# A fused decoder layer: mask order, small differences and key sums in its first attention

## The reference

```python
def _feature_map(t, K):
    f = jnp.einsum('hdf,bhld->bhlf', K, t)
    feats = jnp.concatenate([jax.nn.softmax(f, axis=-1), jax.nn.softmax(-f, axis=-1)], axis=-1)
    return jnp.maximum(feats, EPS)          # EPS = 1e-12

def _L0_attn_ref(x, Wq, Wk, Wv, Wo, Kq, Kk):   # 16 heads of 64
    q, k, v = _heads(x @ Wq), _heads(x @ Wk), _heads(x @ Wv)
    qf, kf = _feature_map(q, Kq), _feature_map(k, Kk)
    kv = jnp.cumsum(kf[:, :, :, None, :] * v[..., None], axis=2)
    o = jnp.einsum('bhlf,bhldf->bhld', qf, kv)
    z = jnp.einsum('bhlf,bhlf->bhl', qf, jnp.cumsum(kf, axis=2)) + EPS
    return (o / z[..., None]).transpose(0, 2, 1, 3).reshape(B, L, H * HD) @ Wo

x = x + _L0_attn_ref(_layernorm(x), ...)
x = x + _L0_xattn_ref(_layernorm(x), ctx, mask, ...)
x = x + _L0_ffn_ref(_layernorm(x), ...)
```

## Time and profile before

| | us |
|---|---|
| median of 2 runs | 1312.96 (1311.81 and 1314.12) |
| the profiled execution | 1310.69 |
| its span, first to last instruction | 1308.5 |
| the steady loop of the first attention in it | about 86 to 598 |

### The profile page before, as it was taken

The page is one execution under the profiler, slowest core; times in us unless marked ns, Lnnn a source line. Parts: engine busy times, 40 slices in busy tenths (PEclk is TensorE's granted clock), DMA queues, the critical chain, the costliest instruction groups (busy, mean ns, idle before and its releaser), DMA issues. The chain is left out here.

```text
span 1308.5 us, 30248 instructions
## 1 busy us (share of the span) xinstructions
PE 1151.0 (88%) x11860; PEld 755.3 (58%) x11861; DVE 934.6 (71%) x1705; ACT 645.9 (49%) x1230; POOL 528.8 (40%) x477
## 2 busy tenths in 40 slices
PE   6688795888778898888899999999999975999996
PEld 6577675777667786776334434433444332666665
DVE  6867775776646766667877977787788746677766
ACT  3333343333333343333577867776778852444443
POOL 4464477455644455551331032023100134566651
PEclk9888898888988898999999999999999987999998
DMA  6100002000040000022284058017322017121125
GB/s 226 38 7 2 2 2 73 2 1 1 1 75 2 1 2 1 2 35 43 75 142 88 8 91 153 2 29 125 74 85 116 2 51 201 50 64 64 60 61 196
DMA packets 60046, 73.66 MB, mean 56 GB/s; under 512 B 14404, under 2 KB 51140, under 8 KB 59188
## 3 DMA queue, kind: packets, MB, share of 16 engines
q1 hardware_dynamic: 56132, 61.56, 19.7%
q0 software_dynamic: 3792, 10.36, 2.6%
HBM read 52.86 MB, written 18.78 MB: 55 GB/s over the span
## 5 line engine op out<-in xcount | busy, mean ns | idle before, releaser
L1751 ACT ACTIVATE pt<-pR 128x512 f32<-128x512 f32 x512 | 286.2, 600 | 76.2 <-PE pR L1642 71.3
L1836 DVE TENSOR_REDUCE neg_max<-pS 128x1 f32<-128x1024 f32 x238 | 284.8, 1219 | 52.5 <-PE pS L1619 52.4
L1642 PE MATMUL pR<-qs,ks 100*32 100x512 bf16 x2048 | 190.1, 381 | 2.6 <-ACT pt L1751 1.6
L1619 PE MATMUL pS<-ks,qs 100*32 100x512 bf16 x1904 | 144.9, 378 | 4.8 <-DVE neg_max L1836 1.8
L1656 PE MATMUL b_pO<-pt,b_v 128*32 128x512 f32 x1024 | 134.2, 598 | 2.9 <-ACT pt L1751 2.3
L1498 POOL COPY qs<-max_rows 3x512 bf16<-3x512 bf16 x60 | 36.5, 609 | 209.1 <-ACT max_rows L1744 206.0
L352 POOL TENSOR_TENSOR am<-am,a_causal 128x512 f32<-128x512 f32 x64 | 82.6, 1291 | 70.9 <-ACT am L793 70.9
L1642 PEld LDWEIGHTS pR<-qs,ks 100*32 100x32 bf16 x2048 | 55.9, 96 | 94.1 <-issue 23.9
L543 PE MATMUL pO<-v,am 128*64 128x66 f32 x1024 | 64.5, 237 | 34.4 <-POOL am L352 34.4
L1619 PEld LDWEIGHTS pS<-ks,qs 100*32 100x32 bf16 x1904 | 51.2, 96 | 72.9 <-issue 35.4
L540 PE MATMUL pO<-state,qfT 128*64 128x66 f32 x768 | 52.0, 233 | 39.6 <-POOL am L352 39.4
(11 more groups left out here) (380 smaller groups left out, 2530.2 us busy)
## 6 DMA issues: line engine op xcount, KB each, us to landing
qs<-q_scr SPq DMA_DIRECT2D x24, 256.0 KB
ks<-k_scr SPq DMA_DIRECT2D x7, 768.0 KB
k_scr<-f SPq DMA_DIRECT2D x18, 256.0 KB, 3.0
ks<-in_L_ffn_w_dram SPq DMA_DIRECT2D x2, 2048.0 KB, 11.1
ks<-in_L_ffn_w_dram SPq DMA_DIRECT2D x4, 1024.0 KB, 9.1
ks<-y_rows SPq DMA_DIRECT2D x16, 256.0 KB, 5.0
ks<-k_scr SPq DMA_DIRECT2D x6, 512.0 KB
cx<-in_ctx_dram SPq DMA_DIRECT2D x3, 768.0 KB, 13.0
```

Source lines behind the costliest of these rows:

```text
L1619: ins = pe.matmul(pS1[q:q + XV, slot, 512 * half:512 * half + 512], qs[0:KR, bass.ds(par, 1), h, P * t + q:P * t + q + XV].rearrange("r a ...
L1642: ins = pe.matmul(ring[bank][q:q + XV, :], ks[0:KR, bass.ds(par, 1), h, P * j + q:P * j + q + XV].rearrange("r a n -> r (a n)"), qs[0:KR, ...
L1751: nc.scalar.activation(pt[:, j % 2, i, :], ring[bank], ACT.Exp).then_inc(exp_done, 1)
L1836: nc.vector.tensor_reduce(neg_max[:, hg % 2, u // G, u % G:u % G + 1], pS1[:, u % 2, :], AX_X, ALU.max, negate=True).then_inc(max_done, 1)
```

## The change

The diff has three parts, all in the first attention.

1. GpSimd runs mask(t, 3) directly behind mask(t, 2), ahead of the scaling of the next tile's queries.
2. The subtraction minimum less maximum (128x8) moves from VectorE to GpSimd, where it stands in front of each negative side, behind the same wait on `drained`. The negative side waits for it through a semaphore of GpSimd's own, `s_apart`.
3. `denominators` reduces the key sums in two halves of 8 heads, from the second tile on, the first as soon as the first half's exponentials are there. Both are counted by VectorE's chain, so that `DVE_BATCH` becomes 76. The reciprocal stays one.

```diff
--- before.py
+++ after.py
@@ -176,6 +176,7 @@
         y_done, x1_done = sem("y_done"), sem("x1")
         x1_stats, x1_norm = sem("x1_stats"), sem("x1_norm")
         s_c, s_on = sem("c"), sem("on")
+        s_apart = sem("apart")
         s_split, s_rows, s_aug = sem("split"), sem("rows"), sem("aug")
         s1_done, max_done = sem("s1"), sem("max")
         c_turned = sem("c_turned")
@@ -212,7 +213,7 @@
 
         ROUNDS = 8
         WARM = 16
-        DVE_BATCH = 72
+        DVE_BATCH = 76
         HALVES = (slice(0, H // 2), slice(H // 2, H))
         POOL_FROM = (2, 1)
 
@@ -334,10 +335,14 @@
                     nc.gpsimd.tensor_tensor(e, e, d.unsqueeze(2).broadcast_to([P, d.shape[1], HD]),
                                             ALU.mult).then_inc(scaled[m], 1)
 
+                apart = Chain(pool, s_apart)
+
                 def other_side(m, t, half_of, par):
 
                     pool.wait_ge(drained[m], 2 * (t - POOL_FROM[m]) + half_of + 1)
                     hs = slice(8 * half_of, 8 * half_of + 8)
+                    apart.did(nc.gpsimd.tensor_tensor(low_less_high[:, m, hs], lo[:, m, hs], hi[:, m, hs], ALU.subtract))
+                    apart.wait()
                     nc.gpsimd.tensor_tensor(feat[m][:, par, hs, HD:F2],
                                             low_less_high[:, m, hs].unsqueeze(2).broadcast_to([P, H // 2, HD]),
                                             feat[m][:, par, hs, 0:HD], ALU.subtract).then_inc(shifted[m], 1)
@@ -411,9 +416,9 @@
                         if (b, c) == (0, 0):
                             constants()
                         mask(t, 2)
+                        mask(t, 3)
                         if has1:
                             scale(1, t + 1, 1 - par)
-                        mask(t, 3)
                         if (b, c) == (0, TB - 1):
                             split_k(0)
                             split_k(1)
@@ -968,8 +973,6 @@
                     own.did(nc.vector.tensor_reduce(hi[:, m, hs], f, AX_X, ALU.max))
                     own.did(nc.vector.tensor_reduce(lo[:, m, hs], f, AX_X, ALU.min))
                     own.wait()
-                    if t >= POOL_FROM[m]:
-                        nc.vector.tensor_tensor(low_less_high[:, m, hs], lo[:, m, hs], hi[:, m, hs], ALU.subtract)
                     ins = nc.vector.tensor_tensor(feat[m][:, par, hs, 0:HD], f,
                                                   hi[:, m, hs].unsqueeze(2).broadcast_to([P, H // 2, HD]),
                                                   ALU.subtract)
@@ -981,12 +984,14 @@
                                             ALU.subtract).then_inc(shifted[m], 1)
 
                 def denominators(m, t, par, own, hs=slice(0, H), part=1):
-                    wait(dve, expd[m], 2 * t + part + 1)
                     if t:
                         wait(dve, scaled[m], t + 1)
                     d = fsum[:, m, 2 * hs.start:2 * hs.stop]
-                    own.did(nc.vector.tensor_reduce(
-                        d, feat[m][:, par, hs].rearrange("p h (s f) -> p (h s) f", s=2), AX_X, ALU.add))
+                    for half_of, now in enumerate(HALVES if t and m == 0 else (hs,)):
+                        wait(dve, expd[m], 2 * t + (half_of if t and m == 0 else part) + 1)
+                        own.did(nc.vector.tensor_reduce(
+                            fsum[:, m, 2 * now.start:2 * now.stop],
+                            feat[m][:, par, now].rearrange("p h (s f) -> p (h s) f", s=2), AX_X, ALU.add))
                     own.wait()
                     nc.vector.reciprocal(d, d).then_inc(summed[m], 1)
```

## The result

The changed kernel takes 1239.3 us (median of 2 runs, 1235.69 and 1242.9) against 1312.96 us: a ratio of 0.944 (95% interval 0.932 to 0.956). The forecast was 1237 us. Run again beside other kernels it took 1238.8 us, ratio 0.944 (0.939 to 0.949). The profiled execution took 1235.7 us.

The account below looks back on a forecast made before the run. TensorE bounds, held up in the first attention by GpSimd's mask and half clock. 42.1 + 30.6 + 3.6 + 1.4 + 1.3 - 3 = 76.0 us less gives 1237 us; range 1226 to 1250.

Parts of the forecast that it names:

- Last mask ahead of the scaling: First attention: GpSimd's last mask before the query scaling removes 13 TensorE waits, 42.1 us, and the scaling loses nothing.
- Rival 3: Last score copy waits on ScalarE behind the second query exponential, so waits shrink only a third: about 1298 us; chance 0.05.
- The clock: TensorE's half clock after 11 of the 13 last-mask waits goes away, 2.78 us each: 30.6 us.
- rival 1: The clock does not come back, as TensorE still waits 0.92 us a tile: 1268 us; chance 0.12.
- the third masks: TensorE's waits for the third mask, 2.6 us in three tiles, shrink by half: 1.3 us.
- small new waits: 3 us set against the gains, as 0.3 us more on GpSimd meets slacks of that size.
- The small subtraction: GpSimd's moved 128x8 subtraction with its wait takes 0.3 us, four a tile, within the slacks.
- Rival 2: Small subtractions near their upper end, or scaling, clamp and key chain, become the bound: 28 us back, 1265 us; chance 0.15.
- Rival 4: Slower: all four GpSimd subtractions a tile stand behind VectorE's port-holding work and are exposed: 1354 us; chance 0.03.
- The power: In three tiles the second mask's wait behind the second norm's power shrinks from 1.97 to about 0.8 us: 3.6 us.
- Splits: In the fourth tile, bounded by GpSimd's split work, the mask leaves the way before it: 1.4 us.
- Key sums by halves: Key sums come 1.1 us earlier but gain nothing in a steady tile, as GpSimd's first mask ends later.

Follow-up runs that it names:

- order_only: The kernel before with only the first part of the diff, the last mask ahead of the query scaling: 1249.7 us, ratio 0.951.
- rows_moved: The changed kernel with VectorE's second key mask row and four row normalisations each one group later: 1236.9 us, ratio 0.944.
- rows_and_splits: The changed kernel with VectorE's mask row and row normalisations one group later and GpSimd's split work spread over idle places: 1223.3 us, ratio 0.933.
- splits_spread: The changed kernel with GpSimd's split work spread over idle places in other tiles: 1233.9 us, ratio 0.942.

## Why the prediction was right, point by point

- *Last mask ahead of the scaling, 42.1 us.* Right. All 13 waits are gone; the mask ends before the sums in the tile shown, and the scaling lost nothing. Rival 3 is out: the last score copy stands on ScalarE behind the second query exponential, as it feared, but this is done at 266.13, before the scores themselves are (266.40), and the sums need it too and then 2.3 us of reduction.
- *The clock, 11 x 2.78 = 30.6 us.* Right in mechanism and nearly in size. Kept busy through the old waits, the old kernel gains 27.2 us. In the steady tile, 12.85 us became 10.13, against a forecast of 10.07. The 0.92 us wait of each tile does not bring the clock down, so rival 1 is out: 0.97, not 0.89.
- *Order together.* order_only measured 65 us where the terms for it (42.1 + 30.6 - 3) give 69.7. The 1.3 us for the third masks is not the order's: those waits stay there (1.08, 1.10 and 0.88 us) and go only with the moved work. The third, sixth and fifteenth tile gained 5.2, 1.9 and 3.7 us, 9 us less than the terms give them.
- *The step that failed.* I wrote that no more than 3 us of small new waits would come, and laid them on GpSimd's subtractions. They were elsewhere and larger: in the third and sixth tile the waits for the last mask went and with them most or all of the half clock, but VectorE's mask row and row normalisations now stood before a remainder for which TensorE was ready earlier. TensorE waits 2.82 and 3.19 us for it instead of 0.93, in the third tile with 3.4 us of half clock behind it. With this the third and the sixth tile gained 4.45 and 4.24 us, where the forecast's terms give 7.5 (4.4 of wait, 2.8 of clock, 0.3 of the third mask) and 7.6 (3.6, 2.8, and 1.2 at the power). In the kernel before the same collision was there (a mask row of 3.19 us), hidden under the wait for the last mask. The fifteenth tile, whose TensorE then waits for VectorE's first maxima (1.45 us, with 3.4 us of half clock), gained 3.4 instead of 6.4 us; in rows_moved, with the same wait and no half clock, it is 27.33 us instead of 28.99. I had looked for the next wait in a steady tile only.
- *The small subtraction, 0.3 us.* Right: 0.20 us alone, and 0.08 from its end to the start of the negative side. The collision with the clamp came once in 13 of the tiles, as weighed, and the negative side gave back what the subtraction lost. Rival 2 is settled by the repeated subtraction: it needed the upper end, and at that end its 28 us do appear (29 us). Rival 4's exposure of all four is out: 1.6 of 4.5 us come in.
- *The power, 3 x 1.2 us.* The number came, the mechanism did not. Against order_only the tenth and fourteenth tile are 30.19 and 30.18 us instead of 31.56 and 31.69, 1.4 and 1.5 us. The wait for the mask did shrink, from 1.95 to 0.66 us in the tenth tile, but the wait of 1.21 us for the key copies took its place. What the tile gained is the 3.4 us of half clock that stood behind the wait of 1.95 us. The forecast had neither the new wait nor this half clock: it counted 11 half-clock stretches, and in the kernel before there are two more, behind the power's waits of 1.94 and 1.95 us (at 400.1 to 403.4 and 540.1 to 543.4 the clock is 0.50).
- *Splits, 1.4 us.* The fourth and fifth tile together gained 6.5 us, where the terms give 7.0 (2.8 of wait, 2.8 of clock, 1.4).
- *What I gave nothing.* The first tile gained 3.5 us: its third mask's wait fell from 4.64 to 2.84 us, and the half clock at it from 6.8 to 3.4 us.
- *Key sums by halves, nothing in a steady tile.* Right in number (27.76 and 27.79 us). The reason given, that the first mask ends behind the sums anyway, no longer holds in the shorter tile, where without the halves the scaling waits 0.18 us for the sums; the slack on the key side hides this.

So the sum of 76.0 us against 75.0 owes something to luck: three tiles gained 9.4 us less than the terms give, where 3 us were set aside, and against that stand the 3.5 us of the first tile and 3.6 us spread over nine others, less 1.5 us in the fifth and the ninth. The 3.6 us of the power came by another way than forecast.

## What to carry to other kernels

An engine's order written by hand should be checked for a ready instruction standing behind one that is not; here one swapped pair was worth 65 us of 1313. In the kernel before, a wait of 2.8 to 4.4 us on TensorE cost its own length and the half clock behind it, 2.5 us more for each of 11 waits. After a wait is taken out, go through the tiles that are not like the others: small work that the wait had hidden is what is late next.

## What the runs showed of the hardware that was not expected

The same wait is not always followed by the half clock. In the sixth tile TensorE waited 3.19 us in the changed kernel and 3.21 us without the halves; the first went on at full clock, the second ran about 7 us at half clock, and its tile is 2.9 us longer. The first tile took 31.40, 32.85, 32.88 and 34.02 us in four profiled executions whose kernels don't differ there (rows_and_splits, rows_moved, the changed kernel run again, splits_spread). Waits near 2 us went either way too. In the kernel before those of 1.94 and 1.95 us were followed by 3.4 us of half clock and those of 1.97 and 1.82 us were not; in order_only all three (1.97, 1.95 and 2.06 us) were. So part of the differences of 2 to 5 us between these kernels is the clock's, not the edit's, and their medians should be read with the tiles beside them.
